# Rows normalised earlier, bias products later, and dense filler multiplies in front of two stages of a mixture-of-experts kernel

## What is computed

```python
h = _layernorm(x) * (1 + ca) + sa                  # x: 4 x 1024 x 256; sa, ca, ga, sb, cb, gb from silu(c) @ wmod
q, k, v = unit_projection(h @ W.T + b)             # three times: FFT, divided by its magnitude
s = cumsum(bind(k, v), axis=1)                     # product of spectra, running sum over the sequence
x = x + ga * unbind(s, q)
h = _layernorm(x) * (1 + cb) + sb
y = experts(h)                                     # 8 experts, top 2 of 8 by h @ gate_w, swiglu, 256 -> 1024 / 512 -> 256
x = x + gb * y
```

## Time and profile before

| what | us |
|---|---|
| median of 3 runs | 601.66 (601.19 to 602.39) |
| the profiled execution, whole | 599.83 |
| its span, first to last instruction | 597.8 |
| mean granted TensorE clock | 0.940 |
| TensorE / VectorE / ScalarE / GpSimd busy | 545.0 / 476.3 / 294.5 / 293.6 |

### The profile page before, as it was taken

How to read it: one execution, slowest core, us unless ns; L and a number is a source line. 1 busy time by engine, 2 the same in 40 slices (tenths; PEclk the granted TensorE clock), 3 DMA queues, 4 the chain that set the end, 5 groups by cost and what they waited for, 6 DMA issues and landing times.

```text
span 597.8 us, 12946 instructions
## 1 busy us (share of the span) xinstructions
PE 545.0 (91%) x3923; PEld 407.1 (68%) x3924; DVE 476.3 (80%) x1058; ACT 294.5 (49%) x497; POOL 293.6 (49%) x197
## 2 busy tenths in 40 slices
PE   5999899999999995847799999999999999999992
PEld 4545455647555563525488888888888888888771
DVE  1258889899999989999678888888888888888762
ACT  3676679687886954542443333333333333333330
POOL 0002232423433242100548888788888888877532
PEclk9799989798998997757799999999999999999998
DMA  9305453645456344934467777877777777755632
GB/s 309 119 2 193 106 176 92 190 106 159 124 180 174 104 142 112 347 109 74 111 138 128 131 135 140 130 141 133 136 138 138 129 132 132 137 95 88 115 38 27
DMA packets 81570, 79.30 MB, mean 133 GB/s; under 512 B 44596, under 2 KB 71348, under 8 KB 81272
## 3 DMA queue, kind: packets, MB, share of 16 engines
q0 software_dynamic: 16912, 31.74, 30.2%
q1 hardware_dynamic: 63320, 46.15, 27.5%
q10 hardware_dynamic: 1296, 0.87, 0.5%
HBM read 44.06 MB, written 22.23 MB: 111 GB/s over the span
## 4 chain that ended last, share of the span: by engine, by line
PE 63%; DVE 22%; issue 5%; ACT 4%; DMA 3%; POOL 2%; POOLq 0%; DVEq 0%; ACTq 0%
PE ps L761 31%; PE ps L782 15%; PE ps L517 7%; PE ps L576 3%; DVE region L1229 2%; POOL region L1631 1%; DVE region L1193 1%; PE ps L616 1%; DVE region L1276 1%; PE ps L612 1%; DVE region L1373 1%; DVE region L1244 1%; DMA region<-in_dft 1%; DMA region<-region 1%; PE ps L530 1%
## 5 line engine op out<-in xcount | busy, mean ns | idle before, releaser
L761 PE MATMUL ps<-region,w_sb 128*128 128x256 f16 (+1 forms) x1872 | 201.8, 265 | 2.2 <-issue 2.1
L761 PEld LDWEIGHTS ps<-region,w_sb 128*128 x1872 | 173.2, 98 | 25.8 <-issue 3.5
L1661 POOL DMA_INDIRECT out_rows<-w_stage,region x71 | 135.0, 1901 | 50.5 <-issue 19.8
L1651 POOL DMA_INDIRECT region<-h_scratch,region x71 | 95.8, 1349 | 70.3 <-DVE region L1510 45.0
L1542 DVE TENSOR_SCALAR region<-ps,region 128x256 f32<-128x256 f32 (+1 forms) x156 | 64.2, 455 | 55.9 <-PE ps L761 52.2
L782 PE MATMUL ps<-region 128*128 x852 | 99.5, 273 | 3.3 <-DVE region L1556 3.2
L1102 ACT ACTIVATE region<-ps,region 128x256 f32<-128x256 f32 (+1 forms) x156 | 62.2, 451 | 79.7 <-PE ps L761 74.4
L1114 ACT ACTIVATE region<-region 128x1024 f16<-128x1024 f32 (+1 forms) x39 | 38.3, 981 | 110.2 <-DVE region L1550 100.7
L782 PEld LDWEIGHTS ps<-region 128*128 128x128 f16 x852 | 82.5, 98 | 14.4 <-issue 4.1
L517 PE MATMUL ps<-region 128*128 128x512 f32 x192 | 86.0, 605 | 3.9 <-ACT region L875 3.9
L1631 POOL TENSOR_TENSOR region<-region 128x512 f32<-128x512 f32 x30 | 37.3, 1275 | 100.5 <-DVE region L1256 100.5
(11 more groups left out here) (224 smaller groups left out, 691.9 us busy)
## 6 DMA issues: line engine op xcount, KB each, us to landing
w_stage<-in_w SPq DMA_DIRECT2D x20, 512.0 KB, 4.3
region<-in_x SPq DMA_DIRECT2D x8, 512.0 KB, 8.0
out_rows<-region SPq DMA_DIRECT2D x8, 512.0 KB, 3.3
h_scratch<-gb_bc SPq DMA_DIRECT2D x4, 1024.0 KB, 7.1
h_scratch<-region SPq DMA_DIRECT2D x8, 512.0 KB, 3.2
region<-region POOLq DMA_DIRECT2D x7, 512.0 KB, 6.0
region<-in_ramp SPq DMA_DIRECT2D x1, 2064.0 KB, 11.3
region<-in_w SPq DMA_DIRECT2D x4, 512.0 KB, 6.3
```

Source lines behind the costliest of these rows:

```text
L761: mm = pe.matmul(ps[:, GV + 2 * half + a, (f % 2) * MT:(f % 2) * MT + wide], w, xg_t[:, s, xa * KD + k, 0:wide], start=(n == 0), stop=(n = ...
L1651: G.indirect_dma_start(out=xg_rows[:, t % XG, u, :], out_offset=None, in_=h_scratch, in_offset=bass.IndirectOffsetOnAxis(ap=gather_idx[:, ...
L1661: G.indirect_dma_start(out=out, out_offset=bass.IndirectOffsetOnAxis(ap=scatter_idx[:, at:at + 1], axis=0), in_=y_sb[:, t % 2, u, :], in_o ...
```

## The change

1. VectorE's stream begins with one memset of zeros (`warm`, in a buffer that the first block uses later), and TensorE multiplies them 18 times (512 columns, float16, into bank 3) ahead of `transform_weights`. Three more stand behind the transposes of `project(0)`.
2. The bias products move from ahead of those transposes to behind them (and behind the three).
3. TensorE's transposes wait for two copied weights, no longer for all six, the scales and the biases. `transform(0)` waits for six weights and the scales at its first product, and for the biases at its third.
4. ScalarE makes the square root behind the first copied weight, the normalised rows behind the second, then weights 3 and 4, the scales, weights 5 and 6, `spectra(0)`, the biases, and only then `project(1)`.
5. At the turn to the experts TensorE has 8 multiplications of the identity with a piece of the first expert weights (512 columns, float16, into bank 5) ahead of `first_rows(0)` and 3 more behind it. The results of all these products are overwritten unread.

```diff
@@ -200,6 +200,7 @@
         wmod_sb = z_flat[:, 6 * NB:6 * NB + 6 * BLK].rearrange("p (k n) -> p k n", k=KD)
         mod_rows = h2_rows.bitcast(F32).rearrange("p j d -> p (j d)")[0:BATCH, :].rearrange("b (m d) -> b m d", m=4)
         mod_tmp = s_flat[0:BATCH, 0:2 * D].rearrange("b (m d) -> b m d", m=2)
+        warm = sq.rearrange("p c r n -> p (c r n)")[:, 0:(P + BLK) // 2].bitcast(FP16)
         wraw = m_flat[:, 0:3 * KD * D].rearrange("p (c k d) -> p c k d", c=3, k=KD)
         dft_sb = uk[:, :, :].rearrange("p r n -> p (r n)")[:, 0:KD * NF].rearrange("p (k f) -> p k f", k=KD)
         alt_rep = den[:, 0:P]
...
@@ -446,6 +447,11 @@
         @block.tensor
         def _(pe):
+            def keep_warm(n, w, cols, bank):
+
+                for _ in range(n):
+                    pe.matmul(ps[:, bank, :], w, cols, start=True, stop=True)
+
             def transform_weights():
                 pe.wait_ge(wraw_in, 32)
...
@@ -456,6 +462,9 @@
                                            dft_sb[:, ke, :], start=(ke == 0), stop=(ke == KD - 1))
                         mm.then_inc(pe_setup, 1)
                 scale_columns()
+
+            def bias_products():
+
                 pe.wait_ge(bq_in, 32)
                 for r in range(3):
                     for ke in range(KD):
...
@@ -498,8 +507,7 @@
                 pe.wait_ge(n_ready, TPB * (t + 1))
                 if t == 0:
                     pe.wait_ge(ident_in, 16)
-                    pe.wait_ge(act_setup, 7)
-                    pe.wait_ge(sca_copied, 1)
+                    pe.wait_ge(act_setup, KD)
                 if t >= 1:
                     pe.wait_ge(ht_ready, KD * t)
                 if t >= 4:
...
@@ -511,6 +519,11 @@
                 for i in range(6):
                     c, r = i // 2, i % 2
                     bank_free(pe, ("z", t, i))
+                    if t == 0 and i == 0:
+                        pe.wait_ge(act_setup, 3 * KD)
+                        pe.wait_ge(sca_copied, 1)
+                    if t == 0 and i == 2:
+                        pe.wait_ge(act_setup, 3 * KD + 1)
                     for k in range(KD):
                         if i == 0:
                             pe.wait_ge(ht_ready, KD * t + k + 1)
...
@@ -675,10 +688,14 @@
                                    start=(c % PC == 0), stop=(c % PC == PC - 1))
                 mm.then_inc(perm_mm, 1)
+            pe.wait_ge(warm_set, 1)
+            keep_warm(18, warm[:, 0:P], warm[:, P:], 3)
             transform_weights()
             for t in range(-1, NBLK):
                 if t == -1:
                     project(0)
+                    keep_warm(3, warm[:, 0:P], warm[:, P:], 6)
+                    bias_products()
                     transform(0)
                     nyquist_cols(0)
                     modulation_rows()
...
@@ -799,7 +816,9 @@
             pe.wait_ge(tiles_ready, 4)
             e = experts(0)
+            keep_warm(8, ident_h[:], w1_sb[:, HI, 0:BLK], GV + 1)
             first_rows(0)
+            keep_warm(3, ident_h[:], w1_sb[:, HI, 0:BLK], GV + 1)
             up(0, 0, e[0], None, between=lambda: first_rows(1))
             for i in range(2):
                 pe.wait_ge(w_lo[i], W_CHUNKS)
...
@@ -828,16 +847,16 @@
             act.wait_ge(c_in, 16)
             nc.scalar.activation(c_sig, c_sb, ACT.Sigmoid).then_inc(sig_done, 1)
-            def weights_in():
-                for n in range(6):
-                    act.wait_ge(pe_setup, n + 1)
-                    nc.scalar.activation(w_spec[:, n // KD, n % KD, :], ps[:, n, 0:NF], ACT.Copy).then_inc(act_setup, 1)
-                    if n == 3:
-                        project(0)
-                        normal_rows(0)
+            def weight_in(n):
+                act.wait_ge(pe_setup, n + 1)
+                nc.scalar.activation(w_spec[:, n // KD, n % KD, :], ps[:, n, 0:NF], ACT.Copy).then_inc(act_setup, 1)
+
+            def scales_in():
                 act.wait_ge(sca_mm, 1)
                 nc.scalar.activation(sca_t.rearrange("p w k b -> p (w k b)"), ps[:, 7, 0:4 * BATCH],
                                      ACT.Copy).then_inc(sca_copied, 1)
+
+            def bias_in_columns():
                 act.wait_ge(pe_setup, 7)
                 nc.scalar.activation(bias_f, ps[:, 6, 0:9], ACT.Copy).then_inc(act_setup, 1)
...
@@ -1013,9 +1032,18 @@
                 act.wait_ge(g_ready, 2 * (t + 1))
                 nc.scalar.activation(prod[0:1, 0, IM, 0:BLK], rot(("row", t, 0))[0:1, :], ACT.Copy).then_inc(row_ready, 1)
-            weights_in()
+            weight_in(0)
+            project(0)
+            weight_in(1)
+            normal_rows(0)
+            for n in (2, 3):
+                weight_in(n)
+            scales_in()
+            for n in (4, 5):
+                weight_in(n)
+            spectra(0)
+            bias_in_columns()
             project(1)
-            spectra(0)
             normal_rows(1)
             for t in range(-1, NBLK):
                 if t + 1 < NBLK:
...
@@ -1146,6 +1174,7 @@
         @block.vector
         def _(dve):
             V = nc.vector
+            V.memset(warm, 0.0).then_inc(warm_set, 1)
             V.memset(eps_col, EPS_LN)
             V.memset(ny_run[:, 0:1], 0.0)
             V.memset(z[:, 0, :, IM, BLK:NB], 0.0).then_inc(ny_zero, 1)
```

More of the change, by code:

```diff
@@ L307, in adaln_moe_kernel @@
         (route, w_exp, perm_mm, tiles_ready, w_sub, top_max, top_idx, ramp_in, early_ready, base_ready, late_ready,
-         late_mm, rank_mm, lo_made, hi_made, row_made, first_tp, first_x) = (
+         late_mm, rank_mm, lo_made, hi_made, row_made, first_tp, first_x, warm_set) = (
             sem(n) for n in ("route w_exp perm_mm tiles_ready w_sub top_max top_idx ramp_in early_ready base_ready "
-                             "late_ready late_mm rank_mm lo_made hi_made row_made first_tp first_x").split())
+                             "late_ready late_mm rank_mm lo_made hi_made row_made first_tp first_x warm_set").split())
         (l_idft, l_x2, l_stats, l_agg, l_std, l_rstd, l_mid, l_h2, l_hi, l_lo, l_tp, l_ht, l_gate, l_gates) = (
```

## The result

The changed kernel takes 594.12 us (median of 3 executions, 593.98 to 594.50) where the kernel before takes 601.66: a ratio of 0.9869, 95% interval 0.9832 to 0.9905, or 7.5 us less. Forecast were 4.9 us less, and a range down to 595.4. The same kernel was run in three later sets beside the other experiments: over all 21 executions its median is 594.5, its mean 595.3 (standard error 0.6), and single executions lie between 592.0 and 601.8. The kernel before has a mean of 602.1 over 96 executions (standard error 0.15), 599.3 to 607.0. So the better number for the change is 6.8 us, standard error 0.6. One of the 21 executions, that of 601.78, is more than 1.5% above the fastest and counts as a slow run; without it the mean is 594.9 and the change is worth 7.1 us.

What follows compares the result with a forecast made beforehand. TensorE, 63% of the chain that ended last, was taken as the bound. Start -5.0 and turn +0.1 made -4.9: profiled 599.83 to 594.9, plus 1.83 for the median, 596.8; range 595.8 to 598, for 8 in 10 595.4 to 600.2.

Steps and rivals of the forecast that it cites:

- the last term of the sum: Whole kernel: the median of the runs lies 1.83 us above the profiled execution, taking 594.9 to 596.8.
- The filler and the weights: Start of TensorE: eighteen multiplies by zeros end at 7.0, weights then take 5.22 us, not 6.84; 0.4 us late allowed.
- the bound of 0.8: Start of TensorE: with a late rise of the clock the filler ends at most about 0.8 us late.
- The rival of zeros: Start and turn: zeros don't raise the clock, the filler runs late, kernel slower at 605.2 us; chance 0.05.
- ScalarE's new order: Start: normalised rows ready at about 13.3, not 17.05; block 1's rows and the later evacuate(0) cost zero.
- `transform(0)`: First transform on TensorE: starts at 17.2, not 20.63, takes 10.26 us, not 12.24, ends at 27.5: 5.4 us earlier.
- the rival with 0.25: Start: the clock falls all the same before the first transform, the start gives only 2.3 us, time 599.5; chance 0.25.
- The sum at the start: Start to first transform's end: 5.4 us earlier, less 0.4 for the filler's late rise, so minus 5.0.
- The turn: Turn to the experts: eight products cost 1.75, three nothing, 1.66 comes back in the first half of up(0); net plus 0.1.
- They cost their full 8 x 0.218 = 1.75 us: Turn to the experts: the gather is already there, so the eight products ahead of the transposes lie wholly on the path.
- The range: Whole kernel: forecast's own range 595.8 to 598 us; for 8 in 10, over the fallen clock, 595.4 to 600.2.
- The shift is partly lost in the first half: Blocks or turn: low clock falls elsewhere or the turn's 1.66 doesn't return, costing 1 to 2.5 us, 598.5; chance 0.13.

Runs made afterwards that it cites:

- the start alone: Changed kernel without the 8 and 3 filler products at the turn to the experts; medians 597.62, 595.36 and 596.83 us in three sets.
- the order alone: Changed kernel with no filler product at all, only the new order of ScalarE's and TensorE's work at the start; 599.33 us, ratio 0.9959.
- the filler alone: Kernel before, old order, with only the memset and the eighteen multiplies by zeros ahead of the weights; 601.73 us, ratio 0.9978.

## Why the prediction was right and wrong

- **The step that failed: the last term of the sum.** The forecast for the profiled execution was 594.9, and it took 594.50. To this the prediction added "the median of the runs lies 1.83 above it", as if the distance that the kernel before had between its profiled execution and its median of three were a constant. In the changed kernel the median of three lies 0.4 below the profiled execution (594.12 against 594.50). Of the 2.6 us between 596.8 and 594.12 this term is 2.2, and all the rest of the sum 0.4. The 1.83 was a draw: the profiled 599.83 is among the fastest of 96 executions of before, whose mean is 602.1, while over 21 executions the changed kernel's mean lies 0.8 us above its profiled one.
- **Luck in the 0.4.** The profiled pair differs by 5.3 us: 5.5 at the first magnitudes and 0.8 in the blocks, less 0.8 at the turn and 0.1 behind it. The sum had 5.0 for the start, nothing for the blocks and 0.1 lost at the turn, so blocks and turn were both missed and cancelled. Of the 5.5, 0.3 us is the transform's table landing earlier (6.97, not 7.24), which the change did not bring about.
- **The filler and the weights.** Forecast: begins at 1.4, ends at 7.0, nothing lost, 0.4 us late on average. Measured: 1.27 to 6.64, and in the other traces to between 6.7 and 8.2; L461 starts 0 to 1.0 late. The size is right, 0.3 to 0.4 late on average; the bound of 0.8 is passed in the three with the latest rise. The weights take 5.4 to 5.5 us, forecast 5.22.
- **The rival of zeros** that don't raise the clock is refuted: eighteen slow passes would take 7.7 us, they took 5.4 to 6.9, and the weights behind them ran at the full clock.
- **ScalarE's new order.** Rows ready at 12.7, forecast 13.3; the moments of block 1 begin at 15.31, forecast 15.6; `evacuate(0)` begins at 20.66, and catches up before the last product, as forecast.
- **`transform(0)`.** Forecast 17.2 to 27.5, measured 16.85 (16.99 in the chain) to 27.4. The clock held in all 13 profiled executions with fillers and the new order; the rival with 0.25 did not occur in any, and it did in the one trace of the new order without fillers. Its chance was set too high. The prediction compared how much wide work stood behind the narrow passes in blocks where the clock fell and blocks where it held; but the trace of before has the same sixteen transposes and then the same wide passes behind them in both (106.8 and 160.2), and the transposes take longer where the clock fell. The amount of work was not what told them apart. The three zeros that the prediction weighed in were not needed in either trace without them.
- **The sum at the start:** forecast 5.0, and 5.46 in the first magnitudes; the runs of the start alone give 5.2 (mean 596.9 against 602.1, standard error 0.4). The Trainium skill's rule ("TensorE: Matmul & The Clock Gate", Part 1) that the point of the rise varies from run to run is borne out by the filler's 5.4 to 6.9 us. The page gives 0.5 us either way. The traces show more: with 0.21 us lost for each slow pass, an estimate from these lengths is that the filler had run for 3 to 6 us when the clock rose.
- **The turn:** forecast +0.1, and in the old order it is -0.1 (standard error 0.3) by the runs and 0.0 in the trace (12.05 and 12.02 us). Behind the new start a second step fails: "They cost their full 8 x 0.218 = 1.75 us". The products ahead of the turn (L600) run in part at half the clock there in 11 of 12 traces, ScalarE comes late, and a part of the 1.75 lies in a wait. Against the new start without them the fillers give 1.6 us (standard error 0.7) by the runs, and 0.7 on the mean of the traces. The prediction also had nothing for the turn being about 1.2 us longer behind the new start.
- **The range.** The low end of 595.4 allowed for the price of each step, and took a difference between two medians as if it had no scatter of its own. "The shift is partly lost in the first half" allowed for a loss in the blocks, not for a gain, and the changed kernel's blocks gave 0.8 us in the profiled pair. One execution of the changed kernel has a standard deviation of 2.7 us, of before 1.4; with medians of three, a draw of 1.5 us either way is usual. Of the 7.5 us measured first, 5.2 are the start, 0.7 to 1.6 the turn, and what is left, about 1, is of the size of that draw. It can't be settled further with these executions. With it in the range the low end would have been near 593.

## What to carry to other kernels

Price an edit on the clock by the executions and not by one trace: one profiled execution shows one draw, its distance from the median is no constant to be carried to the next kernel, and the range has to hold the draw of both kernels beside the prices of the steps. Filler that keeps the clock is best put where the engine waits, though here moving the turn's filler there brought nothing in the runs (596.7 against 595.3). By the runs the order alone brought half of what the new start did, and the filler alone nothing that is clear of the scatter; at the full clock from its beginning the first transform ran only with both. Before putting an engine's delay on the path, look at whether the engine that takes over from it is already late.

## What the runs showed of the hardware

- Products of zeros raise the clock: 18 passes of 512 columns took 5.4 to 6.9 us where all at 1.2 GHz would take 7.7, and the 24 passes of 257 columns behind them took 5.4 to 5.5 us, not 7.0.
- The profile's PEclk is 1.00 in the first 8 us of every trace, also where the passes are slow: in the trace of before L455 took 6.84 us and PEclk is 1.00 from 7 to 14 us.
- The execution varies by more than the rows around a change suggest: the same blocks took 250.4 us in one and 256.9 us in another. In all seven executions with a granted clock of 0.89 between 120 and 150 us the blocks were longer than in the eleven with 0.94 or 1.00. Three of the seven had the latest rise at the start; the others did not.
- Three more wide products in each block (4.6 us in all) neither raised the mean clock (0.940) nor narrowed the spread.
